# Reordered units of a selective scan, with the rows of B and C written to all partitions from SBUF by one transfer a row

## The reference

```python
hidden = rmsnorm(residual, norm_w[i])
xz = hidden @ in_w;  u, z = split(xz, 2)
uc = silu(conv1d(u) + cb)                    # 4 taps, causal
x_dbl = uc @ xp_w                            # dt (16), B (16), C (16) for every token
dt = softplus(dt_r @ dt_w + dt_b)
A = -exp(A_log)                              # 128 channels x 16 states
def step(h, inp):
    u_t, dt_t, B_t, C_t = inp
    h = exp(dt_t[..., None] * A) * h + (dt_t * u_t)[..., None] * B_t[:, None, :]
    y_t = einsum('bds,bs->bd', h, C_t)
    return h, y_t
y = (scan(step) + u * D) * silu(z)
hidden = y @ out_w
```

## Time and profile before

| | us |
|---|---|
| median of 3 runs (383.53 to 384.74) | 383.85 |
| the profiled execution | 383.59 |
| its span, first to last instruction | 381.8 |
| DVE busy | 285.5 |
| ACT busy | 236.2 |
| POOL busy | 195.9 |

### The profile page before, as it was taken

One profiled execution on the slowest core, in us unless ns is written; L12 is line 12 of the kernel. 1 busy time (PEld: TensorE's weight loads), 2 busy tenths in 40 slices (PEclk: granted clock), 3 DMA queues, 4 the chain that ended last, 5 costly groups with the idle time before them and its releaser, 6 DMA issues.

```text
span 381.8 us, 5717 instructions
## 1 busy us (share of the span) xinstructions
PE 329.2 (86%) x1904; PEld 233.6 (61%) x1904; DVE 285.5 (75%) x496; ACT 236.2 (62%) x674; POOL 195.9 (51%) x175
## 2 busy tenths in 40 slices
PE   4866998899989999689989889898898989878684
PEld 3354875556548547466667666676766767656562
DVE  2674477989764543599998989889898998988363
ACT  1103278887870664786877867777686877863163
POOL 2989200000000410397887968888696887967000
PEclk9995699999996899999999999999999999995968
DMA  7960400000000030635427163461725527160000
GB/s 212 364 119 3 124 2 1 2 2 1 3 0 2 5 108 0 212 127 218 169 110 274 33 250 113 164 231 51 278 67 211 162 116 278 34 245 0 1 2 14
DMA packets 19751, 41.07 MB, mean 108 GB/s; under 512 B 7986, under 2 KB 10626, under 8 KB 19594
## 3 DMA queue, kind: packets, MB, share of 16 engines
q1 hardware_dynamic: 19434, 40.38, 31.0%
q10 hardware_dynamic: 288, 0.33, 0.3%
HBM read 40.31 MB, written 0.39 MB: 107 GB/s over the span
## 4 chain that ended last, share of the span: by engine, by line
PE 52%; DVE 28%; ACT 9%; issue 6%; POOL 3%; DMA 1%; DVEq 0%; SPq 0%; POOLq 0%; ACTq 0%
DVE big L1182 14%; PE PS L708 5%; PE PS L521 4%; DVE big L1192 3%; PE PS L661 3%; PE PS L700 3%; PE PS L297 2%; PE PS L485 2%; ACT PS L1487 2%; PE PS L415 2%; PE PS L732 2%; PE PS L585 2%; PE PS L291 2%; PE PS L495 2%; PE PS L622 2%
## 5 line engine op out<-in xcount | busy, mean ns | idle before, releaser
L1182 DVE TENSOR_TENSOR_SCAN big<-PS,big 128x1024 f32<-128x1024 f32 x48 | 109.6, 2287 | 5.6 <-ACT PS L1487 5.2
L1487 ACT ACTIVATE PS<-unit_t,amat 128x255 f32<-128x255 f32 x192 | 82.5, 467 | 20.7 <-DVE unit_t L1157 16.6
L1702 POOL TENSOR_TENSOR big<-big 128x1024 f32<-128x1024 f32 (+1 forms) x48 | 86.2, 1821 | 3.1 <-DVE big L1182 2.4
L1691 POOL TENSOR_TENSOR big<-unit_t,big 128x1024 f32<-128x1024 f32 x24 | 57.1, 2381 | 17.9 <-DMA big<-spill 17.9
L694 PE MATMUL PS<-big,cst 128*128 128x256 f32 x192 | 50.1, 407 | 1.3 <-POOL big L1702 1.2
L1658 POOL TENSOR_TENSOR w2t<-w2t,w0t 128x768 f32<-128x768 f32 x2 | 3.6, 1821 | 88.8 <-DVE big L1116 88.8
L694 PEld LDWEIGHTS PS<-big,cst 128*128 128x128 f32 x192 | 37.6, 201 | 8.1 <-POOL big L1702 2.6
L1298 ACT ACTIVATE big<-PS 128x512 f32<-128x512 f32 (+1 forms) x43 | 24.7, 583 | 22.5 <-PE PS L521 7.4
L1350 ACT ACTIVATE big<-PS,big 128x256 f32<-128x256 f32 x64 | 29.7, 474 | 1.5 <-DVE big L956 1.4
L1173 DVE TENSOR_TENSOR big<-unit_t,PS 128x1024 f32<-128x1024 f32 x24 | 29.0, 1208 | 1.7 <-PE PS L661 0.6
L661 PE MATMUL PS<-stack,pick_b 96*128 96x256 bf16 x144 | 22.2, 277 | 7.5 <-DVE big L1173 4.0
(11 more groups left out here) (336 smaller groups left out, 663.2 us busy)
## 6 DMA issues: line engine op xcount, KB each, us to landing
big<-spill SPq DMA_DIRECT2D x60, 512.0 KB, 5.9
w3t<-in_w SPq DMA_DIRECT2D x1, 1588.0 KB, 13.6
big<-routed SPq DMA_DIRECT2D x8, 128.0 KB, 2.9
w2t<-in_w SPq DMA_DIRECT2D x1, 896.0 KB, 9.8
cst<-in_const SPq DMA_DIRECT2D x1, 848.0 KB, 7.7
w5t<-in_w SPq DMA_DIRECT2D x1, 812.0 KB, 6.0
w2t<-in_wm SPq DMA_DIRECT2D x1, 768.0 KB, 4.7
w1t<-in_w SPq DMA_DIRECT2D x1, 385.0 KB, 8.2
```

Of the source, the lines that this page charges most:

```text
L1182: v.tensor_tensor_scan(flat(hst[:, g]), flat(da[g % 2]), flat(dbu[:, g]), 0.0, ALU.mult, ALU.add).then_inc(sem("m_h"), 1)
L1487: one = act.activation(da[g % 2][:, n, 1:N], dt[u % 2][:, 1:N], ACT.Exp, scale=amat[:, u // 2, col:col + 1])
L1691: pool.tensor_tensor(dbu[:, g], dtu[b].unsqueeze(1).to_broadcast([P, SG, N]), bsp[b][:, SG * (g - 2):SG * (g - 1)], ALU.mult).then_inc(sem ...
L1702: pool.tensor_tensor(hc[:, g, s:s + size], hst[:, g, s:s + size], csp[u % 2][:, SG * g + s:SG * g + s + size], ALU.mult).then_inc(sem("m_h ...
```

## The change

The store to spill, SP's wait for it and the five loads of a unit are gone. In their place SP issues 20 transfers, one for each row: the source is one row of xds, named 128 times by a step of zero, the destination the same 1 KB stretch of all 128 partitions. Four transfers share a semaphore, so POOL waits for 64 where it waited for 16.

The order of the work in a unit is changed too. On PE, the z projection leaves prep_in and becomes prep_in_z; sum_y takes any states of any group and waits for each half of a group by itself; sum_skip moves ahead of spread_second, the first state of group 0 and prep_in ahead of spread_last. On ACT, the decays of groups 1 to 3 lie differently between the steps of the preparation, and the third part of stack's split (prep_part) is one step earlier. On POOL, weigh 0 and weigh 1 are done in halves (weigh 2 was before), so m_hc counts six a unit. DVE has the same order; the count that it waits for follows m_hc.

```diff
                 sp.wait_ge(sem("m_xs"), 4 * u + 1)
-                sp.dma_start(spill[b], xds[b][2 * SG:7 * SG, :]).then_inc(sem("st_B"), 16)
-                sp.wait_ge(sem("st_B"), 16 * (u + 1))
                 for g in range(5):
                     to = bsp[b][:, SG * g:SG * (g + 1)] if g < 2 else csp[b][:, SG * (g - 2):SG * (g - 1)]
-                    sp.dma_start(to.rearrange("p s n -> p (s n)"),
-                                 spill[b, SG * g:SG * (g + 1)].rearrange("s n -> (s n)").partition_broadcast(P))\
-                        .then_inc(sem(f"ld_B{b}{g + 2}" if g < 2 else f"ld_C{b}{g - 2}"), 16)
+                    for n in range(SG):
+                        row = SG * (g + 2) + n
+                        sp.dma_start(to[:, n], xds[b][row:row + 1].unsqueeze(1).to_broadcast([1, P, N]))\
+                            .then_inc(sem(f"ld_B{b}{g + 2}" if g < 2 else f"ld_C{b}{g - 2}"), 16)
...
+            def prep_in_z(u):
+
+                i, b = divmod(u, 2)
                 pe.matmul(zps, inz[:, i], ht[b][0:64, 3:3 + N], start=(u == 0), stop=True, skip_group_check=True)\
                     .then_inc(sem("m_in"), 1)
...
+            def sum_y(u, g, some):
+
+                for s in some:
+                    if g < NSG - 1:
+                        pe.wait_ge(sem("m_hc"), 6 * u + 2 * g + s // 2 + 1)
+                    else:
+                        pe.wait_ge(sem("m_hc3"), 2 * u + s // 2 + 1)
+                    last = pe.matmul(yps, ident, hc[:, g, s], start=False, stop=True, skip_group_check=True)
                 return last
...
+                sum_y(u, 2, (0, 1))
+                sum_y(u, 3, (0,))
+                sum_y(u, 2, (2,))
                 if more:
                     spread_first(u + 1)
-            sum_last(UNITS - 1)
-            sum_third(UNITS - 1, 1).then_inc(sem("m_y"), 1)
+                sum_y(u, 2, (3,))
+                sum_y(u, 3, (1, 2, 3)).then_inc(sem("m_y"), 1)
...
-                pool.wait_ge(sem(f"ld_B{b}{g}"), 16 * (u // 2 + 1))
+                pool.wait_ge(sem(f"ld_B{b}{g}"), 64 * (u // 2 + 1))
...
-                weigh(u, 0)
+                weigh(u, 0, 2)
                 drive(u, 3)
-                weigh(u, 1)
+                weigh(u, 1, 2)
                 weigh(u, 2, 2)
```

More of the change, by code:

```diff
@@ L686, in sum_skip @@
                 pe.matmul(yps, dmat[:, i], uc[b], start=True, stop=True)
[L688 to L700, removed]
-                return last
[L703 to L708, removed]
+            def sum_y(u, g, some):
[5 more added lines that the diff above has]
+                    last = pe.matmul(yps, ident, hc[:, g, s], start=False, stop=True, skip_group_check=True)
+                return last
             def out_proj(u):
@@ L739, in _ @@
             prep_in(0)
+            prep_in_z(0)
             keep_awake(3)
@@ L749, in _ @@
                 if u:
-                    sum_last(u - 1)
-                    sum_third(u - 1, 1).then_inc(sem("m_y"), 1)
                     out_proj(u - 1)
+                sum_skip(u)
                 spread_second(u)
-                sum_skip(u)
                 if more:
@@ L757, in _ @@
                     prep_transpose(u + 1)
+                sum_y(u, 0, (0,))
+                if more:
+                    prep_in(u + 1)
                 spread_last(u)
                 if more:
-                    prep_in(u + 1)
+                    prep_in_z(u + 1)
                     prep_x(u + 1)
-                sum_y(u, 0, u + 1 if more else None)
+                    pe.wait_ge(sem("m_zs"), u + 2)
+                sum_y(u, 0, (1, 2, 3))
+                sum_y(u, 1, (0,))
                 if more:
                     take_away(u + 1, 0)
-                sum_y(u, 1)
+                sum_y(u, 1, (1, 2, 3))
                 if more:
                     take_away(u + 1, 1)
-                sum_third(u, 0)
+                sum_y(u, 2, (0, 1))
+                sum_y(u, 3, (0,))
+                sum_y(u, 2, (2,))
                 if more:
                     spread_first(u + 1)
-            sum_last(UNITS - 1)
-            sum_third(UNITS - 1, 1).then_inc(sem("m_y"), 1)
+                sum_y(u, 2, (3,))
+                sum_y(u, 3, (1, 2, 3)).then_inc(sem("m_y"), 1)
             out_proj(UNITS - 1)
@@ L1180, in scan @@
                 if u and g < NSG - 1:
-                    v.wait_ge(sem("m_hc"), 4 * (u - 1) + (g + 1 if g < 2 else 4))
+                    v.wait_ge(sem("m_hc"), 6 * (u - 1) + 2 * g + 2)
                 v.tensor_tensor_scan(flat(hst[:, g]), flat(da[g % 2]), flat(dbu[:, g]),
@@ L1471, in prep_softplus @@
                 act.activation(sp_a, dtp, ACT.Abs).then_inc(sem("m_sp"), 1)
+                prep_part(u, 1)
                 act.wait_ge(sem("m_sp"), 4 * u + 1)
@@ L1474, in prep_softplus @@
                 act.activation(sp_u, sp_a, ACT.Exp, scale=-1.0, bias=logs_t).then_inc(sem("m_sp"), 1)
-                prep_part(u, 1)
                 act.wait_ge(sem("m_sp"), 4 * u + 2)
@@ L1506, in _ @@
                 decay(u, 0, every)
-                decay(u, 1, every[0:3])
+                decay(u, 1, every[0:2])
                 if u:
@@ L1513, in _ @@
                     keep_residual(u - 1)
-                decay(u, 1, every[3:4])
+                decay(u, 1, every[2:3])
                 if u and more:
                     prep_hs(u + 1)
+                decay(u, 1, every[3:4])
                 decay(u, 2, every[0:1])
@@ L1519, in _ @@
                     prep_ht(u + 1)
-                decay(u, 2, every[1:3])
+                decay(u, 2, every[1:4])
                 if more:
                     prep_tu(u + 1)
-                decay(u, 2, every[3:4])
+                decay(u, 3, every[0:1])
                 if more:
                     prep_zs(u + 1)
-                decay(u, 3, every[0:2])
+                decay(u, 3, every[1:3])
                 if more:
                     prep_xd(u + 1)
-                decay(u, 3, every[2:4])
+                decay(u, 3, every[3:4])
                 if more:
@@ L1694, in weigh @@
             def weigh(u, g, parts=1):
-                pool.wait_ge(sem(f"ld_C{u % 2}{g}"), 16 * (u // 2 + 1))
+                pool.wait_ge(sem(f"ld_C{u % 2}{g}"), 64 * (u // 2 + 1))
                 pool.wait_ge(sem("m_h"), u * NSG + g + 1)
```

## The result

The changed kernel takes 1165.63 us (median of 4 runs, 1163.9 to 1170.42) beside 383.69 for the kernel before (four runs, the three named ahead and one more): a ratio of 3.041, 95% interval 3.028 to 3.054. The profiled execution took 1163.9 us, its span is 1162.1.

What follows compares the result with a forecast made beforehand. Before: a ring of DVE, PE, ACT and POOL, DMA beside it; after, one-lane transfers. 153.7 + 2 + 1160 + 33.2 = 1349, with the profiled execution's excess over its span 1351 us; range 374 to 1440.

Steps and rivals of the forecast that it cites:

- That the transfers decide and the order hides: Units: in the slow case every wait the new order shortens hides behind C2, so its worth is nothing.
- One lane, 27.1 GB/s, 4.84 us a row: Row transfers from xds: each passes one lane, a sixteenth of the full DMA rate, 131,072 bytes in 4.84 us; chance 0.60.
- 12 x 96.7 us: Twelve units' row transfers: 20 x 4.84 = 96.7 us a unit, without gaps, 1160 us in all.
- the second rival: Row transfers: reads spread in part, two to five lanes at once, 48 to 20 us a unit, 767 to 430 us; chance 0.08.
- One engine or one partition: Row transfers: one engine carries each, or all 16 meet at one partition; sign: 1 or 16 small packets a transfer.
- The rest of the sum: Outside the units' transfers: first issue at 153.72 us, about 2 us until engines move, 33.2 us from C2's landing to the end.
- The signs named: DMA and POOL: landings tens of us after issue, near 27 GB/s, big<-xds waits about 80 us a unit, units 97 us apart.
- One sign of being wrong: DMA engines during a unit: a busy share of half or more would show the forecast wrong.
- The order: PE, ACT and POOL in the units: shorter waits before gate and last scan, -3.9 to -7.2 us if transfers keep up.
- a cost that was called hidden: POOL's C0 and C1 in halves: 0.4 us a unit, hidden by POOL's idle time; uncovered, 5 us.
- That fits: SP's issues: 20 at 0.5 us each are 10 us of a unit's 16.34.
- the slow end: Row transfers: all of a transfer passes through one lane, 25.9 to 28.3 GB/s, instead of costing nothing.

Runs made afterwards that it cites:

- The kernel that never changes lane: Changed kernel with all 20 transfers of a unit reading the same one row, partition 8; 1351.01 us, one run.
- the copies 32 and 64 partitions away: Two kernels: changed kernel with every second row of a group read from xds's equal copy 32 or 64 partitions further; 1165.12 us with 32, 746.95 with 64.

## Why the prediction was right, point by point

- **That the transfers decide and the order hides**: right. The transfers alone give 1169.58, the order alone 376.99; in the changed kernel the order's gain does not show.
- **One lane, 27.1 GB/s, 4.84 us a row**: right as the price of a lane. The kernel that never changes lane took 1351.01 us against a forecast of 1351, at 27 GB/s throughout.
- **12 x 96.7 us**: the mis-sized term. The sum took a unit's 20 rows as 20 times the lane's time. A unit took 80.2 us in the stretch shown and 81.3 on the mean (first issue at 152.71, C2 of the last unit taken up at 1128.27), because the five groups lie in five lanes and the engines overlap two lanes at each border, 16.5 us in the unit shown and 15.4 on the mean. That is the second rival, spreading in part, in a small dose; it had been weighed as a case of its own instead of as a correction to the first. It makes the 185 us between forecast and result. The time fell into the stated range, but the changed kernel is not the case of 20 full prices that the forecast was summed for.
- **One engine or one partition**: left open ahead of the result, now settled. 16 small packets a transfer, and the copies 32 and 64 partitions away, show sixteen engines at one lane, and a lane wider than a partition.
- **The rest of the sum**: the start (153.72 forecast, 152.71), the end from C2 on (33.2 forecast, 33.8 from 1128.27 to 1162.1) and the claim that the next unit's rows are always queued held: from 155 us to the last rows the DMA engines have no idle slice.
- **The signs named**: a late landing (14.9 us after the issue by the median, tens named) and POOL's waits on big<-xds (68 us a unit, 80 named) came as named. Units came some 81 us apart where 97 was named, and the rate over a unit was 33 GB/s where 27 was named: 27 is the rate between the changes of lane. One sign of being wrong came too, a DMA share of half or more in a unit: it stood at 0.79, and was no sign of work.
- **The order**: -3.9 to -7.2 us forecast, -7.8 measured. The gate's wait gave 0.78 us instead of 0.35, the last scan's 0.19 of the 0.3 allowed. Against it stands a cost that was called hidden: POOL's halves, by delaying prep_gz, put 0.46 us on DVE. That leaves 0.51 us of the 0.71 that the beat fell by; the other 0.2 is not accounted for.
- **"That fits", of the 20 issues**: only as a total, and only while the transfers keep up. In the changed kernel an issue took 4.6 us by the median, not 0.5. The run with rows from DRAM shows that with the store ahead of them C0 comes up to 2.5 us late.
- **The evidence used for the slow end**, that 64 partitions took about half the rate of 128, does not carry the choice: no run tested it, and the issues alone may explain it. As far as the rows go there was luck in choosing that end; what the runs bear out is the price, a sixteenth of the full rate.

## What to carry to other kernels

In these runs the side that is read set the rate, at the same bytes and pieces: ask not only how much a transfer moves and in what pieces, but from how many places it reads. A row of SBUF that all partitions need comes back from DRAM, after a store, in an eighth of the time that it takes straight from its partition (some 10 us for a unit's 20 rows against 80); if it must come from SBUF, put copies 64 partitions apart and let neighbours in the queue read different lanes, which halved the loss here and no more (746.95 us, against 1165.63 and 383.69). And hold each transfer's issue and landing against the moment when its own reader wants it, not against the beat of the loop.

## What the runs showed that was not expected

Sixteen engines that read one row keep a busy share of seven to eight tenths while moving 27 GB/s: so the busy share of the DMA engines counts time in which they wait, and only the GB/s row beside it tells that from work. And a store of 20 KB with five loads of 512 KB, 2.6 MB in some 10 us from the store's issue, beat 2.6 MB that never left the core by 70 us a unit.
